# Experts' second layer on one core: rounded weights and their remainders as one moving operand of 512 columns

## The reference

```python
norm = layer_norm(feat, ln_g, ln_b)                       # feat: 8192 tokens x 256
sort_by_expert = balanced_assignment(norm @ centroids.T)  # 1024 tokens for each of E = 8 experts
routed = feat[sort_by_expert].reshape(E, C, D)
h = layer_norm(routed, ln_g, ln_b)
h = gelu(einsum('ecd,edf->ecf', h, w1) + b1[:, None, :])  # F = 1024 hidden
h = einsum('ecf,efd->ecd', h, w2) + b2[:, None, :]        # D = 256
out = routed + h                                          # back in the tokens' order
```

## Time and profile before

| what | us |
|---|---|
| median of 3 runs | 1061.7 (1061.24 to 1061.93) |
| the profiled execution | 1061.36 |
| its span, first to last instruction | 1059.6 |
| PE busy | 1028.2 |
| DVE busy | 815.7 |
| ACT busy | 745.0 |
| POOL busy | 715.9 |

### The profile page before, as it was taken

One profiled execution on the slowest core, in us unless ns is written; L12 is line 12 of the kernel. 1 busy time (PEld: TensorE's weight loads), 2 busy tenths in 40 slices (PEclk: granted clock), 3 DMA queues, 4 the chain that ended last, 5 costly groups with the idle time before them and its releaser, 6 DMA issues.

```text
span 1059.6 us, 20747 instructions
## 1 busy us (share of the span) xinstructions
PE 1028.2 (97%) x7215; PEld 670.6 (63%) x7215; DVE 815.7 (77%) x1858; ACT 745.0 (70%) x966; POOL 715.9 (68%) x753
## 2 busy tenths in 40 slices
PE   5889999999999999999999999999999999999997
PEld 4445555554554454455454443698889999988997
DVE  8999896788788788778777785786777677687861
ACT  3678888888888888888888888755555545455540
POOL 5677878776767767677677657666557676765434
PEclk9999999999999999999999999999999999999999
DMA  4644744444443543533534446153434344452313
GB/s 150 206 153 140 236 161 163 146 155 139 161 148 132 184 148 119 202 128 131 190 121 150 169 161 234 37 147 51 127 53 112 86 90 103 83 126 49 66 21 40
DMA packets 83529, 138.18 MB, mean 130 GB/s; under 512 B 9808, under 2 KB 35792, under 8 KB 83408
## 3 DMA queue, kind: packets, MB, share of 16 engines
q1 hardware_dynamic: 54560, 103.09, 28.7%
q0 software_dynamic: 12288, 16.79, 9.6%
q10 hardware_dynamic: 16560, 16.78, 4.8%
HBM read 86.28 MB, written 50.33 MB: 129 GB/s over the span
## 4 chain that ended last, share of the span: by engine, by line
PE 88%; DVE 6%; issue 2%; ACT 2%; POOL 1%; POOLq 0%; ACTq 0%; DVEq 0%
PE pv L509 19%; PE W L1489 17%; PE S L1475 17%; PE S L494 14%; PE W L453 9%; PE W L478 5%; PE W L464 4%; DVE xb L789 2%; ACT prob L710 1%; PE R L423 1%; PE R L1461 1%; PE pv L1461 1%; DVE raw L844 1%; PE R L434 0%; PE R L552 0%
## 5 line engine op out<-in xcount | busy, mean ns | idle before, releaser
L710 ACT ACTIVATE prob<-S 128x1024 f32<-128x1024 f32 x512 | 496.3, 1023 | 90.0 <-PE S L494 88.8
L509 PE MATMUL pv<-prob,v 128*17 128x512 f32 x2048 | 246.7, 595 | 0.7 <-DVE oT L877 0.7
L494 PE MATMUL S<-stq,stk 64*128 64x512 f32 x1024 | 194.6, 452 | 4.9 <-ACT prob L710 3.3
L494 PEld LDWEIGHTS S<-stq,stk 64*128 64x128 f32 x1024 | 84.4, 184 | 126.8 <-ACT prob L710 107.4
L1752 POOL DMA_INDIRECT out<-prob,order_rows x64 | 105.7, 1651 | 52.4 <-DVE prob L1691 41.4
L509 PEld LDWEIGHTS pv<-prob,v 128*17 128x17 f32 x2048 | 46.0, 96 | 112.1 <-issue 111.3
L1551 ACT ACTIVATE wq_act<-S,b 128x512 f32<-128x512 f32 x64 | 43.9, 685 | 95.2 <-PE S L1475 94.8
L1214 POOL TENSOR_TENSOR sq<-raw 128x512 f32<-128x512 f32 x62 | 64.5, 1041 | 64.8 <-DVE raw L844 42.7
L1475 PE MATMUL S<-raw_nT,xT_w 128*128 128x512 f32 x384 | 91.1, 395 | 0.0
L1244 POOL TENSOR_TENSOR lo<-full,hi 128x512 fp32r<-128x512 f32 x62 | 80.5, 1298 | 5.0
L1475 PEld LDWEIGHTS S<-raw_nT,xT_w 128*128 128x128 f32 x384 | 71.6, 188 | 17.7 <-issue 1.7
(11 more groups left out here) (257 smaller groups left out, 2550.4 us busy)
## 6 DMA issues: line engine op xcount, KB each, us to landing
stk<-parts SPq DMA_DIRECT2D x93, 256.0 KB, 3.6
stq<-parts SPq DMA_DIRECT2D x93, 256.0 KB, 4.6
xT<-in_w SPq DMA_DIRECT2D x32, 512.0 KB, 4.8
parts<-hi SPq DMA_DIRECT2D x63, 256.0 KB, 2.1
parts<-lo SPq DMA_DIRECT2D x63, 256.0 KB, 2.1
out<-ao ACTq DMA_DIRECT2D x32, 256.0 KB, 2.6
xb<-in_x ACTq DMA_DIRECT2D x13, 512.0 KB, 4.6
xb<-in_x SPq DMA_DIRECT2D x2, 512.0 KB, 5.4
```

Source lines behind the costliest of these rows:

```text
L494: ins = e.matmul(S[n % 2][:, h, :], stack["k"][u][64 * h:64 * h + 64, p, c * P:(c + 1) * P], stack["q"][u][64 * h:64 * h + 64, p, :], star ...
L509: ins = e.matmul(pv[32 * j:32 * j + VW, :], v[b % 2][:, c, 8 * u + 4 * g + j, :], prob[(2 * t + j // 2) % RING][:, j % 2, :], start=(c == ...
L710: e.activation(prob[n % RING][:, :, :], S[n % 2][:, :, :], ACT.Exp).then_inc(s_exp, 1)
```

## The change

In each tile of w2, rounded weights and remainders now lie side by side: `w2[i]` holds slices 2i and 2i + 1, each as 256 rounded columns and then 256 remainders. For each chunk and slice the rounded hidden tile is the stationary operand of one matmul over all 512 columns, into the full bank; the hidden remainder multiplies the 256 rounded columns, into the left half. So the bank's left half holds hi x hi + lo x hi, its right half hi x lo. `finish` adds the right half with shift and base into y, waits for that (`f_rest`), and adds the left half. ACT's rounding and DVE's remainders of w2 write two runs of 256 columns with a step. Which memory w2 occupies in sum, the loads and the order of everything else stay.

```diff
-    w2 = [[flat(t[n][i]) for i in range(2)] for n in ("xh", "xl")]
+    w2 = [flat(t[n][i]).rearrange("p (f s d) -> p f s d", f=2, s=2) for n in ("xh", "xl") for i in range(2)]
...
+    f_rest = sem("f_rest")
...
-        for i, (ph, pw) in enumerate(PRODUCTS):
-            ins = e.matmul(down[c % 2][:, 0:D], hid[n % 2][ph][fc][:, c * P:(c + 1) * P],
-                           w2[pw][fc // 4][:, fc % 4 * D:(fc % 4 + 1) * D],
-                           start=(fc == 0 and i == 0), stop=(fc == NFC - 1 and i == 2))
+        both = w2[fc // 2][:, fc % 2, :, :].rearrange("p s d -> p (s d)")
+        tokens = slice(c * P, (c + 1) * P)
+        e.matmul(down[c % 2][:, :], hid[n % 2][0][fc][:, tokens], both, start=(fc == 0), stop=(fc == NFC - 1),
+                 skip_group_check=True)
+        ins = e.matmul(down[c % 2][:, 0:D], hid[n % 2][1][fc][:, tokens], both[:, 0:D], start=False, stop=(fc == NFC - 1),
+                       skip_group_check=True)
...
-    def piece2(m, i):
-        return m[i // 2][:, i % 2 * N:(i % 2 + 1) * N]
+    def rows2(i):
+        return w2raw[i // 2][:, i % 2 * N:(i % 2 + 1) * N].rearrange("p (f d) -> p f d", f=2)
...
-        e.activation(piece2(w2[0], i), piece2(w2raw, i), ACT.Copy).then_inc(f_w2h, 1)
+        e.activation(w2[i][:, :, 0, :], rows2(i), ACT.Copy).then_inc(f_w2h, 1)
...
-        e.tensor_tensor(piece2(w2[1], i), piece2(w2raw, i), piece2(w2[0], i).bitcast(F32), ALU.subtract).then_inc(f_w2l, 1)
+        e.tensor_tensor(w2[i][:, :, 1, :], rows2(i), w2[i][:, :, 0, :].bitcast(F32), ALU.subtract).then_inc(f_w2l, 1)
...
-        e.scalar_tensor_tensor(y[u][:, c, :], down[c % 2][:, 0:D], xshift[n % G][:, c:c + 1], g[n % G][:, c, :],
-                               ALU.add, ALU.add).then_inc(f_y, 1)
+        j = CH * n + c
+        e.scalar_tensor_tensor(y[u][:, c, :], down[c % 2][:, D:2 * D], xshift[n % G][:, c:c + 1], g[n % G][:, c, :],
+                               ALU.add, ALU.add).then_inc(f_rest, 1)
+        e.wait_ge(f_rest, j + 1)
+        e.tensor_tensor(y[u][:, c, :], down[c % 2][:, 0:D], y[u][:, c, :], ALU.add).then_inc(f_y, 1)
```

## The result

The changed kernel takes 1057.8 us (median of 7 runs, 1057.6 to 1058.0), the kernel before 1061.7 (7 runs beside it, 1061.2 to 1062.1): ratio 0.9964, 95% interval [0.9955, 0.9974]. That is 3.9 us or 0.36% faster. At its own limit of 0.2% this is faster, which had chance 0.44, against 0.50 for the same. The gain was forecast at little more than half its size (2.2 of 3.9 us).

A forecast was written before the change was run, and what follows sets the result against it. TensorE's instruction stream was taken to bound the experts' part. Terms: -3.3 (merged matmuls) + 0.6 (transposes' wait) + 0.5 (second add) = -2.2 us, from 1061.36 to 1059.2, plus 0.3 for the median: 1059.5; range 1057.0 to 1062.3.

The forecast's parts named there:

- own limit of 0.2%: Whole kernel: a difference of 0.2%, 2.1 us, is about the least a measurement can tell from none.
- The pair's distance: Second layer: one 512- and one 256-column matmul take 352.3 ns instead of 358.8 for three, saving 3.3 us over 512 groups.
- bounds of 346 and 359: Second layer's group in ns: 345.8 if both sizes cost 12.9 beyond their columns, 358.8 if both cost 19.4.
- warning mark of 348 to 356: Second layer: the forecast is wrong if the pair costs under 348 or over 356 ns.
- rival 2: Second layer: a matmul costs 12.9 ns beyond its columns whatever its length; 4.9 us faster, 1056.8 us; chance 0.16.
- What the transposes take back: Transposes in six even units wait for ACT's scaling, 0.09 us spare; the saving of chunks 0 and 1 is lost, +0.6 us.
- The second add: DVE's finish: a second instruction ends each 0.52 us later, hidden everywhere except at the kernel's end, +0.5 us.
- All three covers: DVE's delay hidden before chunk c + 2 (1.45, 1.7 us spare), the next first layer (0.6 left) and a later split.
- Rival 3: DVE comes late to the next first layer, stopping TensorE 0.3 us in seven units: +2.1, 1061.6 us; chance 0.12.
- The strided writes: ACT's rounding and DVE's subtraction of w2, 32 each, write two runs of 256 with a step at zero extra cost.
- Rival 4: Strided writes slow ACT ahead of even units' transposes: 1.2 us in six units, 7.3 us, 1066.8 us; chance 0.08.
- its spread for the time: Whole kernel: the forecast's own range, 1058.7 to 1060.3 us, from a group saving of 4.6 to 8.4 ns; chance 0.46.

## Why the prediction came out as it did

*The bound.* Right. TensorE's stream sets the experts' part, and every other engine's extra work is covered but in the two places named.

*The pair's distance: the term that was mis-sized.* The prediction took each size's own stream, 6.5 ns a group and 3.3 us in all. The trace gives 4.01 us over 512 groups, 7.8 ns. The handovers between chunks were alike on both sides, so the pair takes 351.0 ns on average, not 352.3. Why it is less than the two pure streams together stays open. The mean hides two kinds: 349 ns in odd units (the stretch of 5.584 us, 16 pairs), 353.4 in even ones. The bounds of 346 and 359 held, and so did the warning mark of 348 to 356. What rival 2 said, 12.9 ns for each matmul, is seen for single ones (226 to 227 ns between long ones in the kernel with long ones first), but is not the mean. The rule of the Trainium skill (TensorE: Matmul & The Clock Gate, Back-to-back issue gap), 2.5 ns a matmul beside its columns, would have given 1.3 us; the page states it for a matmul apart from its weight load. The runs show three times that, with the weight load, at the clock's 2.4 GHz level (granted clock 1.00).

*The first layer.* Left out of the sum, since nothing in it changes; it became 0.35 us shorter, all in the stretches ahead of even units' second layer (11.20 to 11.14). The same code showed 11.20 again with 128 bytes of padding elsewhere. This was not to be had from the rows of before.

*What the transposes take back.* The mechanism was right, in the place and in the six units forecast; the price was too high. The step took the saving of chunks 0 and 1 as lost whole, 0.6 us, because 0.09 us looked like no margin. The wait needs 0.05 (the scaling ends at 892.00 and the load starts at 892.05), so 0.04 of it was free, and six times 0.06, 0.34 us, came about. The pair of runs with POOL's step moved shows that it is this wait. What the step did not have is that chunks 2 and 3 take 0.10 us more in each of these six units than in unit 0, which the 4.01 us of the second layer already contain. Moving POOL's step gave back 0.7 us in all, so that 0.6 comes near the total is luck.

*The second add.* Forecast +0.5, measured +0.46: the second one takes 0.42 us, near the lower bound, not the 0.48 taken. All three covers held; of the 1.23 us ahead of the first layer 0.61 is left, as worked out (0.6). Rival 3 falls.

*The strided writes.* Taken at nothing, and nothing: 620 and 685 ns. Rival 4, the slower side, falls with them.

*The sum.* -2.2 forecast, -3.5 in the traces: 0.7 from the pair, 0.35 from the first layer, 0.3 from the transposes. The forecast's own spread for the pair, a saving of 4.6 to 8.4 ns, held with 7.8; its spread for the time did not, because the other two came on top, and the range held through the room kept for the rivals. The 0.4 us between -3.5 and the -3.9 of the medians is that before's profiled execution was 0.3 us faster than its median and after's 0.1 us slower. All three misses lie on one side, so a forecast on the limit of what can be told became a clear gain.

## What to carry to other kernels

Where TensorE's stream is the bound and its operands stay at 256 columns or more, merging two products with the same stationary tile returns some 8 ns for each matmul saved, weight load included; it takes some sixty of them to pay for the 0.46 us that the merge adds at the end, and over forty more for the transposes' wait. An added instruction on another engine is priced only where nothing covers it: here once out of 64 times. And before a faster stage is counted in full, look for the chain that until now arrived just in time (0.09 us spare here); moving one 0.19 us step out of that chain was worth nothing in the old kernel and over 0.3 us in the new one. Relief has its own edge: giving DVE the third scaling cleared this wait and brought another one within 0.12 us.

## What the runs showed of the hardware

- A stream of matmuls of equal shape has more than one steady distance: the same first layer took 11.14, 11.15, 11.16 or 11.20 us for 48 matmuls, the same pairs 349 to 353.4 ns, by what stands ahead and by an offset of 128 bytes. What selects it stays open.
- Splitting a 256-column matmul in two of 128 costs 101 ns here (behind a long one, a single run); a matmul saved by merging two of 256 returns 8.
- A weight load that waits starts 0.05 us behind the end of ACT's scaling and 0.07 us behind the end of DVE's split. Where that left the first layer's load 0.04 to 0.06 us ahead of its matmul instead of 0.11, the next matmul of 512 columns came 48 to 72 ns late.
- ACT and DVE write 512 elements in two runs with a step as fast as in one run (620 and 685 ns against 620 and 684).
- POOL's power took 2.00 us in even units before and 1.68 when the step behind it was moved ahead, but for one early unit with 2.13 (1.68 in odd units either way; POOL's times in the profile are rough). Why its length changes wasn't followed up.
